# Waits between the routing scatters of the last two batches of a mixture-of-experts layer

## The reference, cut to what matters

```python
x = x + attention(layernorm(x))
logits = layernorm(x) @ router_w + router_b          # 32 experts
topk_p, topk_i = top_k(softmax(logits), 6)           # each token goes to 6 experts
routed = sum over its 6 experts of gate * (relu(f @ w1[e] + b1[e]) @ w2[e] + b2[e])
shared = mean over 2 shared experts of the same form, for every token
x = x + shared + routed
```

## Time and profile before

| | |
|---|---|
| median of 3 runs | 3063.31 us |
| span of the profiled execution | 3108.0 us |
| TensorE matmuls, busy | 2643.3 us (85%) |
| VectorE, busy | 2095.1 us (67%) |
| ScalarE, busy | 1642.7 us (53%) |
| GpSimd, busy | 1403.2 us (45%) |
| DMA queue of SP (q1), share of 16 engines | 41.4% |
| DMA queue of GpSimd (q0), share of 16 engines | 25.7% |

### The profile page before, as it was taken

The page is one execution under the profiler, slowest core; times in us unless marked ns, Lnnn a source line. Parts: engine busy times, 40 slices in busy tenths (PEclk is TensorE's granted clock), DMA queues, the critical chain, the costliest instruction groups (busy, mean ns, idle before and its releaser), DMA issues.

```text
span 3108.0 us, 72648 instructions
## 1 busy us (share of the span) xinstructions
PE 2643.3 (85%) x17832; PEld 1963.1 (63%) x17832; DVE 2095.1 (67%) x4682; ACT 1642.7 (53%) x2863; POOL 1403.2 (45%) x1048
## 2 busy tenths in 40 slices
PE   7799999998966799999478999999898759999992
PEld 5555565555555688888465555555555548888882
DVE  8666676675553678888496666766765527787873
ACT  3255443444412688888432554434444118888882
POOL 3420002214155588888655100032232547888885
PEclk9899999999978899999788999999999879999996
DMA  5876545456567689888759643464474668888888
GB/s 205 210 149 124 129 95 125 118 117 176 160 222 221 128 153 156 153 155 155 146 187 221 127 77 74 94 153 107 119 205 157 229 191 150 156 153 154 153 152 204
DMA packets 292685, 478.75 MB, mean 154 GB/s; under 512 B 55702, under 2 KB 200472, under 8 KB 287176
## 3 DMA queue, kind: packets, MB, share of 16 engines
q1 hardware_dynamic: 198992, 341.60, 41.4%
q0 software_dynamic: 92160, 130.08, 25.7%
q10 hardware_dynamic: 1320, 4.46, 0.9%
HBM read 256.33 MB, written 248.91 MB: 163 GB/s over the span
## 4 chain that ended last, share of the span: by engine, by line
PE 49%; issue 18%; DMA 10%; DVE 9%; POOL 6%; DVEq 3%; POOLq 2%; ACT 1%; SPq 1%; another core or an unknown queue 0%; ACTq 0%; PEldq 0%; PEld 0%
PE ps L1593 11%; PE ps L1607 10%; PE ps L1625 9%; DMA expert_sum<-x,route_u 5%; PE ps L1878 4%; DMA expert_rows<-x 3%; PE ps L1896 3%; POOL expert_rows L1481 3%; PE ps L1611 2%; PE ps L1597 2%; DVE split L1167 2%; PE ps L1670 2%; DVEq L1148 1%; POOLq L376 1%; POOL split L1431 1%
## 5 line engine op out<-in xcount | busy, mean ns | idle before, releaser
L1298 ACT ACTIVATE work<-ps 128x1024 f32<-128x1024 f32 (+3 forms) x768 | 595.4, 809 | 691.4 <-PE ps L1611 441.5
L1481 POOL DMA_INDIRECT expert_rows<-x x372 | 364.8, 981 | 1277.6 <-DVE x L975 615.4
L1508 POOL DMA_INDIRECT expert_sum<-x,route_u x512 | 826.5, 1614 | 197.0 <-issue 92.7
L813 DVE TENSOR_REDUCE small<-ps 128x1 f32<-128x512 f32 (+3 forms) x1216 | 728.8, 656 | 185.3 <-PE ps L1597 105.4
L1593 PE MATMUL ps<-split 128*128 128x512 f32 (+3 forms) x1536 | 512.7, 409 | 53.0 <-DVE work L841 37.6
L1607 PE MATMUL ps<-split 128*128 128x512 f32 (+3 forms) x1536 | 501.4, 406 | 20.2 <-DMA split<-split 16.2
L1878 PE MATMUL ps<-split 128*88 128x256 f32 x3072 | 416.6, 285 | 83.9 <-DVE split L1167 50.1
L1878 PEld LDWEIGHTS ps<-split 128*88 128x88 f32 x3072 | 362.7, 155 | 134.8 <-issue 134.0
L1593 PEld LDWEIGHTS ps<-split 128*128 128x128 f32 x1536 | 276.2, 200 | 251.0 <-DVE small L813 139.7
L1896 PE MATMUL ps<-split 97*128 97x256 f32 x3072 | 409.1, 283 | 3.0 <-DVE split L1182 2.8
L1896 PEld LDWEIGHTS ps<-split 97*128 97x128 f32 x3072 | 384.6, 189 | 3.8 <-issue 3.5
(11 more groups left out here) (178 smaller groups left out, 3159.8 us busy)
## 6 DMA issues: line engine op xcount, KB each, us to landing
x<-expert_rows SPq DMA_DIRECT2D x256, 320.0 KB
split<-qks_scratch SPq DMA_DIRECT2D x180, 256.0 KB
qks_scratch<-split SPq DMA_DIRECT2D x64, 512.0 KB, 4.8
expert_rows<-in_pads SPq DMA_DIRECT2D x65, 320.0 KB, 15.3
xT_scratch<-split SPq DMA_DIRECT2D x16, 1024.0 KB
split<-xT_scratch SPq DMA_DIRECT2D x16, 1024.0 KB
split<-w_scratch SPq DMA_DIRECT2D x6, 1792.0 KB
v_scratch<-work SPq DMA_DIRECT2D x64, 136.0 KB, 4.0
```

The source lines that it names most:

```text
L813: v.tensor_reduce(cols[:, heads[0]:heads[0] + len(heads), i], ps[:, task_bank(n), 0:w * len(heads)].rearrange("p (h k) -> p h k", k=w), AX ...
L1298: c.activation(pexp[:, (s % 2) * 2 + h, :, BLK - w:], ps[:, 2 * h:2 * h + 2, BLK - w:], ACT.Exp).then_inc(s_pe, 1)
L1481: pool.indirect_dma_start(rows, bass.IndirectOffsetOnAxis(ap=posu[b][:, t * 8 + k:t * 8 + k + 1], axis=0), row_tile(b, t // TPB, t % TPB), ...
L1508: pool.indirect_dma_start(acc[r], bass.IndirectOffsetOnAxis(ap=idx[:, j, k:k + 1], axis=0), ye[:, r3, k, :], None, compute_op=ALU.add).the ...
```

## The change

In batches 2 and 3 the stop ahead of each group of eight goes. From the ninth scatter of a batch on, each waits for the landing of the scatter eight places ahead of it, with one wait and one `apart` in front of it. Batches 0 and 1 keep their groups of four, and the wait between two batches stays.

```diff
-                            burst = AHEAD // 2 if b < B - 2 else AHEAD
-                            if n and n % burst == 0:
+                            burst = AHEAD // 2
+                            if b < B - 2 and n and n % burst == 0:
                                 for i in range(n - burst, n):
                                     r, m = divmod(i, TPB * TOPK)
                                     pool.wait_ge(s_disp[r][m % AHEAD], ((L * B + b) * PER + m // AHEAD + 1) * 16)
                                     apart(pool)
+                            if b >= B - 2 and n >= AHEAD:
+                                r, m = divmod(n - AHEAD, TPB * TOPK)
+                                pool.wait_ge(s_disp[r][m % AHEAD], ((L * B + b) * PER + m // AHEAD + 1) * 16)
+                                apart(pool)
                             pool.indirect_dma_start(
                                 rows, bass.IndirectOffsetOnAxis(ap=posu[b][:, t * 8 + k:t * 8 + k + 1], axis=0),
                                 row_tile(b, t // TPB, t % TPB), None).then_inc(s_disp[t // TPB][n % AHEAD], 16)
```

## The result

The changed kernel takes 3021.32 us (median of 4 runs, 3014.81 to 3026.66) against 3063.36 us before, 42.0 us less. The ratio is 0.9855, with a 95% interval of 0.9832 to 0.9879. The profiled execution's span is 3021.4 us, in step with the runs. The span of the profiled execution before, 3108.0 us, was not: that execution was itself some 45 us slower than the median, and the first experiment takes a second profile of the kernel before for that reason.

The account below looks back on a forecast made before the run. GpSimd's last scatter was taken to bound the barrier after phase 2, with SP's weight load late next. Gains of 19.0 us in layer 0 and 14.2 in layer 1, 33.2 together, off 3063.3 gave 3030 us; range 3018 to 3055.

Parts of the forecast that it names:

- rival 4: Start of phase 3: SP's last load is issued earlier, GpSimd alone sets the start; gain 47.9 us, 3015 us; chance 0.09.
- Batch 3's stops go, without a new wait: GpSimd's scatters in batch 3: the last starts 24.6 and 23.4 us sooner by layer; waits already met cost 0.
- The allowance of 9.3 us: Batch 3: a landing may lag its issue by about 9.3 us before GpSimd feels it.
- Batch 2 is worth nothing but the start of batch 3: Batch 2's removed stops: 0 in layer 0, 2.0 us in layer 1, since batch 3 can't start ahead of place_rows.
- What is late next: SP's weight load: End of phase 2: the load of line 488 sets phase 3's start; gains 19.0 and 14.2 us by layer.
- the rule that phase 3 begins about 2 us after the load's end: Start of phase 3: 2 us allowed for the first tile's rows, queued behind the weight load, and TensorE.
- The load's own length: SP's last load: 2640 KB at 398 GB/s take 6.8 us, with 0.9 us until the data flow.
- Rival 1: Batch 3: late landings make GpSimd restart at each scatter, 0.5 us 40 times; gain 8.0 us, 3055 us; chance 0.18.
- Rival 2: Phase 2: SP's transfers wait behind scatters, weight load 23 us later per layer; 3076 us; chance 0.05. Sign: line 488 later.
- Rival 3: GpSimd's scatters: those held back land together, so the stops stay; gain under 6 us, 3060 us; chance 0.06.

Follow-up runs that it names:

- the first experiment: The kernel before, profiled a second time with no edit: 3065.96 us, profiled span 3064.1 us.
- the changed kernel's second run: The changed kernel measured again with no further edit, against the kernel before: 3027.59 us, ratio interval 0.9849 to 0.9904.

## Why the prediction was right, and by how much it was off

The forecast was 3030 us and the measured time 3021.32 us: inside the range, 0.7 us below the forecast's own bounds of 3022 to 3038. The gain was 42.0 us where 33.2 were forecast. What the change removes and adds was right; what would be late next was not, and there the range held only because it reached into rival 4.

- **Batch 3's stops go, without a new wait.** Right. 47 pitches were to take 59.4 and 59.7 us; they took 60.8 and 61.3 us, and one stop of 0.64 us is left. The allowance of 9.3 us, taken from rows with groups, is right to some 0.4 us: a lag of 9.8 us made a stop of 0.64 us, while one of 9.7 us in the changed kernel's second run and one of 9.6 us without the drain and with half the load, both in layer 1, left gaps of 0.40 and 0.31 us. The runs with six and four places bear the rule out.
- **Batch 2 is worth nothing but the start of batch 3.** Right, by the run with batch 2 alone, and the 2 us at the start by the run with batch 3 alone. The prediction gave it to layer 1 only; in the second profile layer 0 has it too, since there place_rows ends before the last landing of batch 2 as well (899.63 against 896.2, released by a landing).
- **What is late next: SP's weight load.** This step failed, in two ways. Its time, "996.95 and 2532.46 whatever GpSimd does", came from one execution that was 45 us slower than the median, and in that stretch SP was 10 and 14 us later after place_rows than in the second profile. I had noted the 44.7 us and spread them evenly over the kernel; they were not spread evenly. Of the 43.9 us between the two profiles of the kernel before, 29.7 us lie ahead of place_rows of layer 0 and 12.6 us between layer 0's first transposes and place_rows of layer 1. Why that execution was slower stays open. A term that says by how much one engine leads another must not be read from such an execution. And the rule that phase 3 begins about 2 us after the load's end, which took the first tile's rows as queued behind it, was wrong in kind: SP issues them only behind the barrier, TensorE begins 16.9 and 16.7 us after line 488 where 9 to 10 were forecast, and halving the load changes nothing, with the drain or without. The load's own length, 7.7 us in the sum, was wrong too: 11.6 and 11.7 us.
- **What stood in its place.** GpSimd set the barrier before and sets it now; the whole of its 23.6 and 18.4 us counted. That is near the amount of rival 4 (47.9 us; the difference is shorter stops in the second profile, a slightly longer pitch and the longer barrier, less the 2 us at layer 0's first scatter), but not its reason: SP's last load does not come sooner because the scatters are gone. It stands 58.5 to 61.6 us after place_rows in every profile but the first, with stops and without them.
- **Rivals 1 to 3.** Rival 1 needs late landings at most waits; of 80 waits in the two batches 3 one made a stop. The run with four places shows some of what it would have looked like. Rival 2 needed SP's last load to slip, by its own sign after the start of phase 2; it stands 129.5 and 128.2 us after that start, against 129.9 and 128.2 us before, although up to eight scatters were in flight all the time. The sentence on the engines' taking turns, from the Trainium skill, page "DMA: Bandwidth & Descriptors", section "Queues, rings and completion order", agrees with that: no transfer of SP stood behind the row of scatters for long enough to move line 488 after line 571 or line 975. Rival 3 fell with the stops.

## What to carry to other kernels

Where one queue issues many transfers and only bounds how many are in flight, let each wait for the one a fixed number of places ahead: the lag of a landing is then hidden as long as it is shorter than that number of pitches less a restart, while a full stop shows the lag of its last transfer every time. Work out the number of places from the longest lag and the restart over the pitch; here 9.8 + 0.8 us over 1.27 us give 8.3, so that eight places leave one short stop, and six or four places gave back 3 to 4 and 13 to 15 us a batch. And before a term rests on how far one engine is ahead of another, see whether the profiled execution is an ordinary one: here a span 45 us over the median of the runs was the sign that it was not.

## What the hardware showed that I had not expected

- The barrier opens 8.9 us after the last scatter's start where the DMA engines' share is 0.00 from 4 us after that start on (both profiles before, batch 2 only, four places ahead), but 9.4 to 9.8 us after it where SP's weight load still keeps the share at 0.76 to 1.06 from 4 to 6 us (changed kernel, batch 3 only, six places ahead, half the load). GpSimd's idle time in the drain is 8.2 and 8.7 to 9.1 us. Without its drain, the barrier opens some 6 us after that start.
- The drain stands in the chain from 956.46 on, while GpSimd still executes scatters until 963.1. I read this as the queue having handed all waits and scatters over five scatters ahead; no run tests it. That a wait in front of a scatter costs nothing when it is met (gaps of 0.30 us with 40 waits a batch) fits that.
- With up to eight scatters in flight all the time the median lag on record in batch 3 was 6.3 and 5.8 us in the changed kernel and 5.3 and 5.4 us in its second run, but 3.4 and 3.1 us in the run without the drain, against 2.9 and 3.0 us in the second profile of the kernel before. Each is taken over a part of the scatters, so that longer lags with more scatters in flight are not shown; SP issued its last load 58.5 to 61.6 us after place_rows in all of them.
